# Attention block on one core: the odd head's queries and keys in six pairs formed from seven block products instead of eight

## The chip, the core and the metric

The kernel runs on one core of a Trainium2 chip. The metric is the device time of that core in microseconds (us). Three runs of the kernel before took 1060.37, 1062.02 and 1061.95 us, median 1061.95. Engines: PE multiplies matrices, DVE (VectorE), ACT (ScalarE) and POOL (GpSimd) work on elements, SP only issues transfers. Each engine executes its own instructions strictly in order and waits on semaphores.

## The reference, cut to what matters

```python
x = hidden_states                       # 2 x 512 tokens, 512 features, float32
n = layernorm(x)
q = rms_norm(n @ Wq + bq, gq)           # 32 heads of 128; the norm is over all 4096 columns
k = rms_norm(n @ Wk + bk, gk)
v = n @ Wv + bv
out = softmax(q k^T / sqrt(128)) v      # by head and batch
x = x + layernorm(out @ Wo + bo)
x = x + layernorm(gated_low_rank_ffn(layernorm(x)))
```

The change touches only `n @ Wq + bq` and `n @ Wk + bk` of some heads, and where sums of n are made.

## The kernel before, in words

Every product is made from float16 halves: a = a_hi + a_lo, and a product is hi x hi + hi x lo + lo x hi, so three matmuls for each 128-row chunk of the features. `xh` and `xl` hold the two halves of the normalised x, features on partitions, 4 chunks x 1024 tokens. Weights of a head (`wa_stage`, 4 slots, query and key) are scaled and split into `wa_hi` (ACT, L1119) and `wa_lo` (DVE, L2222).

The program has two phases. Phase A makes queries and keys of all 32 heads, in 16 pairs of an even and an odd head, and stores them in DRAM with the sums of their squares (`acc`). Phase B does the attention by pair. The norm needs the sums over all heads, so phase B can't begin before phase A is over. In the profile phase A ends near 345 us.

Phase A by head, on each engine (functions `phase_a`):
- PE: four items (`q_or_k`): query and key of batch 0, then of batch 1. An item is 4 chunks x 3 matmuls = 12 matmuls of 128x512 into one PSUM bank; even heads use banks 0 to 3, odd heads 4 to 7. PE waits for the weights (`wa_lo_ready`) and for the bank to be read (`k_out_ready`).
- ACT: for each item the squares; for query items also the scaled query in float32 (`q_s`) and its high half (`qk_out`); before the head, the high halves of the weights two heads on.
- DVE: the scale factors for two heads on (`next_factors`, nine small operations in a chain), the largest weight four heads on (`largest_qk`), the low halves of the weights (`low_wa`), the key of each batch (`store_k`), and the largest of one block of Wv or Wo (`largest_of_unit`).
- POOL: low half of the query (`low_q`) and two additions into `acc` for each batch.
- SP: loads of weights, stores of queries and keys.

Beside this POOL makes, two or four operations to a pair, four sums of blocks of x for phase B (`xs`, kinds XA, XE, XD, XG, each with a high and a low half). Phase B already makes most values from seven block products with them. They are made by pair 13 (36 operations, counted by `x_formed`) and first read in pair 2 of phase B. Nothing in phase A reads them.

Buffers set how far an engine may lag: one `squares` buffer and one `qk_out` buffer for the even head and one for the odd, four weight slots, one PSUM bank to an item.

## Time and profile before

| | |
|---|---|
| median of three runs | 1061.95 us |
| profiled execution | 1060.19 us |
| its span on the core | 1058.4 us |
| PE busy | 1039.7 us, 98% of the span |
| DVE, ACT, POOL busy | 828.2, 764.0, 763.4 us |
| PE idle from 0 to 420 us, longest waits | 1.8, 1.8 and 1.4 us, all in the first 15 us |

The span is the time from the first to the last recorded instruction. A matmul's recorded length (0.38 us) is longer than the distance between two starts, since matmuls overlap; how fast PE works is read from the starts. The same holds on the other engines to a smaller degree: the next start comes about 0.1 us before the recorded end.

### The profile page before, as it was taken

Reading aid. Unit: us, or ns where it says so; the run is one execution under the profiler, and the core shown is the slowest. Engines: PE = TensorE matmul, PEld = TensorE weight load, DVE = VectorE, ACT = ScalarE, POOL = GpSimd, SP = SyncE. Lnnn points to the kernel's source line nnn. Section 1 sums busy time; section 2 is a strip of 40 time slices with the busy share of each in tenths; the row PEclk is TensorE's granted clock in tenths of the full one; section 3 lists DMA queues with packets and bytes.
Section 4 is the critical chain, followed back from the end, with each engine's and each line's share of the span. In section 5 each row is a group of like instructions: output and inputs, shape, how many; then the busy total and the mean of one; then the engine's idle time right before and its main releaser. Section 6 shows DMA issues by size and latency. Waiting matters only on the chain.

```text
span 1058.4 us, 19677 instructions
## 1 busy us (share of the span) xinstructions
PE 1039.7 (98%) x5649; PEld 549.8 (52%) x5649; DVE 828.2 (78%) x1824; ACT 764.0 (72%) x1582; POOL 763.4 (72%) x717
## 2 busy tenths in 40 slices
PE   7999999999999999999999999999999999999997
PEld 4444444444444655556555555555555555555454
DVE  7777876667646778777887987888888888878887
ACT  4666766666647777776788787778787878877756
POOL 2687988788958577765777777778778778767313
PEclk9999999999999999999999999999999999999999
DMA  6678865656574569967667867876877987896702
GB/s 242 176 235 269 254 231 210 227 195 233 201 139 164 178 175 262 250 160 197 149 170 185 195 166 172 200 187 157 203 197 143 216 203 161 224 198 141 177 34 81
DMA packets 312761, 199.91 MB, mean 189 GB/s; under 512 B 275552, under 2 KB 279520, under 8 KB 312672
## 3 DMA queue, kind: packets, MB, share of 16 engines
q1 hardware_dynamic: 304752, 194.24, 68.1%
q10 hardware_dynamic: 7920, 4.62, 1.7%
q8 instruction: 39, 0.64, 0.2%
q14 instruction: 50, 0.41, 0.1%
HBM read 96.03 MB, written 35.68 MB: 124 GB/s over the span
## 4 chain that ended last, share of the span: by engine, by line
PE 87%; DVE 6%; ACT 3%; issue 1%; DMA 1%; POOL 1%; SPq 0%; DVEq 0%; ACTq 0%; POOLq 0%
PE ps L1621 26%; PE ps L1623 25%; PE ps L1622 25%; PE ps L1813 3%; PE ps L1814 3%; PE ps L1815 3%; ACT ps L1301 2%; DVE pair_q L2542 1%; ACT pair_q L1310 1%; DVE y L2555 1%; DMA pair_k<-pair_q 1%; DMA wa_stage<-w_qk 1%; DVE ps L2528 1%; DVE stats L2117 0%; PE ps L1733 0%
## 5 line engine op out<-in xcount | busy, mean ns | idle before, releaser
L1301 ACT ACTIVATE ps<-ps,neg_max 128x512 f32<-128x512 f32 x256 | 168.2, 657 | 57.7 <-DVE ps L2528 57.7
L2542 DVE SCALAR_TENSOR_TENSOR pair_q<-ps,row_inv,pair_q 128x512 f16<-128x512 f32 x256 | 174.2, 742 | 43.8 <-ACT pair_q L1310 40.4
L1621 PE MATMUL ps<-xh,wa_hi 128*128 128x512 f16 x512 | 194.1, 379 | 1.8 <-DVE wa_lo L2222 1.8
L1622 PE MATMUL ps<-xl,wa_hi 128*128 128x512 f16 x512 | 194.1, 379 | 0.0
L1623 PE MATMUL ps<-xh,wa_lo 128*128 128x512 f16 x512 | 194.1, 379 | 0.0
L2528 DVE TENSOR_SCALAR_CACHE_REDUCE ps<-ps,score_down 128x512 f32<-128x512 f32 x256 | 177.1, 753 | 15.2 <-PE ps L1623 14.5
L1310 ACT ACTIVATE pair_q<-ps,row_inv 128x512 f16<-128x512 f32 x256 | 154.5, 689 | 9.0 <-DVE row_inv L2535 8.8
L759 POOL TENSOR_TENSOR acc<-acc,squares 128x512 f32<-128x512 f32 x120 | 151.5, 1284 | 1.6 <-ACT squares L1152 1.6
L1152 ACT ACTIVATE squares<-ps,q_k_bias,qk_down 128x512 f32<-128x512 f32 x128 | 99.1, 785 | 42.9 <-PE ps L1623 28.6
L750 POOL TENSOR_TENSOR qk_out<-q_s,qk_out 128x512 f16<-128x512 f32 x64 | 75.5, 1181 | 52.4 <-ACT qk_out L1161 52.4
L2327 DVE TENSOR_SCALAR qk_out<-ps,k_b,k_g 128x512 f32<-128x512 f32 x64 | 51.8, 809 | 73.9 <-ACT squares L1152 73.8
L905 POOL TENSOR_TENSOR k_lo<-qk_in,k_hi 128x512 f16<-128x512 f32 x62 | 71.7, 1157 | 38.2 <-ACT k_hi L1258 38.1
L1621 PE MATMUL ps<-wo_hi,oth 128*128 128x512 f16 x256 | 97.1, 379 | 1.9 <-issue 0.9
L1621 PE MATMUL ps<-k_hi,qk_in 128*128 128x512 f16 x256 | 97.1, 379 | 1.2 <-issue 0.9
L1623 PE MATMUL ps<-wo_hi,otl 128*128 128x512 f16 x256 | 97.1, 379 | 0.0
L1622 PE MATMUL ps<-wo_lo,oth 128*128 128x512 f16 x256 | 97.1, 379 | 0.0
L1623 PE MATMUL ps<-k_hi,qk_in 128*128 128x512 f16 x256 | 97.1, 379 | 0.0
L1622 PE MATMUL ps<-k_lo,qk_in 128*128 128x512 f16 x256 | 97.0, 379 | 0.0
L1119 ACT ACTIVATE wa_hi<-wa_stage,qk_up 128x512 f16<-128x512 f32 x64 | 42.8, 718 | 75.0 <-DVE qk_up L2174 75.0
L936 POOL CAST oth<-o_t 128x512 f16<-128x512 f32 x62 | 38.3, 618 | 74.0 <-ACT o_t L1275 73.9
L1275 ACT ACTIVATE o_t<-ps,tab 128x512 f32<-128x512 f32 x62 | 42.7, 689 | 58.8 <-PE ps L1623 58.7
L1621 PEld LDWEIGHTS ps<-xh,wa_hi 128*128 128x128 f16 x512 | 50.3, 98 | 61.9 <-issue 2.1
(310 smaller groups left out, 2578.3 us busy)
## 6 DMA issues: line engine op xcount, KB each, us to landing
q_k_scratch<-qk_out SPq DMA_DIRECT2D x64, 512.0 KB, 4.0
qk_in<-q_k_scratch SPq DMA_DIRECT2D x64, 512.0 KB, 3.7
wa_stage<-w_qk SPq DMA_DIRECT2D x32, 512.0 KB, 4.2
u_stage<-w_vo SPq DMA_DIRECT2D x32, 512.0 KB, 5.3
wo_stage<-w_vo SPq DMA_DIRECT2D x16, 512.0 KB, 6.3
x_first<-w_vo SPq DMA_DIRECT2D x12, 512.0 KB, 4.4
qk_tops<-qk_top_scratch ACTq DMA_DIRECT2D x27, 128.0 KB, 3.5
pair_k<-pair_q SPq DMA_TRANSPOSE x130, 4.0
```

The source lines that it names most:

```text
L750: pool.tensor_tensor(pair(qk_out[:, par, b, 1, :])[:, 1, :], q_s[:, par, b * S:(b + 1) * S], pair(qk_out[:, par, b, 1, :])[:, 0, :], ALU.s ...
L759: pool.tensor_tensor(acc[:, w, cols], acc[:, w, cols], squares[:, par, w, cols], ALU.add).then_inc(acc_ready, 1)
L905: pool.tensor_tensor(k_lo[:, s % 2, :], qk_in[:, s, 0, :], k_hi[:, s % 2, :], ALU.subtract).then_inc(qk_lo_ready, 1)
L1152: act.activation(squares[:, par, w, b * S:(b + 1) * S], ps[:, 4 * par + g, :], ACT.Square, bias=q_k_bias[:, par, w:w + 1], scale=qk_down[: ...
L1301: act.activation(ps[:, SCORE + i, :], ps[:, SCORE + i, :], ACT.Exp, bias=neg_max[:, sl, i:i + 1], scale=-1.0, accum_out=row_sum[:, sl, i:i ...
L1310: act.activation(pair_q[:, 0, i, :], ps[:, SCORE + i, :], ACT.Identity, scale=row_inv[:, sl, i:i + 1]).then_inc(high_ready, 1)
L1621: pe.matmul(outp, lhs[0], rhs[0], start=first, stop=False)
L1622: pe.matmul(outp, lhs[0], rhs[1], start=False, stop=False)
L1623: return pe.matmul(outp, lhs[1], rhs[0], start=False, stop=last)
L2327: dve.tensor_scalar(qk_out[:, par, b, 0, :], ps[:, 4 * par + 2 * b + 1, :], k_b[:, slot:slot + 1], k_g[:, slot:slot + 1], ALU.add, ALU.mul ...
L2528: dve.tensor_scalar(ps[:, SCORE + i, :], ps[:, SCORE + i, :], score_down[:, sl, i:i + 1], None, ALU.mult, ALU.min, accum_out=neg_max[:, sl ...
L2542: dve.scalar_tensor_tensor(out=pair_q[:, 1, i, :], in0=ps[:, SCORE + i, :], scalar=row_inv[:, sl, i:i + 1], in1=pair_q[:, 0, i, :], op0=AL ...
```

## The change

**The products.** For the odd head of pairs 9 to 14, [Wk | Wq] is taken as a 2 x 2 block matrix (features 0 to 255 and 256 to 511; the query or the key) and x as 2 x 2 blocks too (features; tokens 0 to 255 or 256 to 511 of each batch). The four output blocks (query and key, first and second half of the tokens) come from seven products of sums of blocks rather than from eight products. A product is 2 chunks x 3 matmuls = 6 matmuls of 128x512. The seven are named C, A, E, B, D, G, F. They accumulate in PSUM banks 4 to 7, and partial results are copied from bank to bank by ACT and added by DVE. Both sums of weights of a formed head use one scale, so its factors are worked out by two dependent operations more.

**The order.** In these pairs the items of the even head lie between the products of the odd one: item, C, A, item, E, B, item, D, G, item, F. All other engines have a new written order for these pairs (`formed_pair`), in which the work of both heads is mixed.

**What each engine does in such a pair that it didn't do before.** POOL: four sums of weights (`formed_sums`, 512, 256, 256 and 256 elements). ACT: a scaled copy of product C to SBUF (`c_q`) and three copies of a bank to a bank, and for the weights one operation of 512 and one of 1280 elements in place of two of 512; two of `q_s` are gone. DVE: two operations that add `c_q` to the query's sums and write `q_s`, and for the weights one of 512 and one of 1280 in place of two of 512.

**The sums of x.** They are now read in pair 9 of phase A, so POOL makes them in pairs 1 to 8, four operations to a pair (30 instead of 36), and DVE makes the first steps of XG beside heads 7 to 11 (four differences of 512 elements and two additions of 512).

```diff
+        FIRST, LAST_PAIR = PAIRS // 2 + 1, PAIRS - 2
+        FORMED_A = LAST_PAIR - FIRST + 1
+        W_SUMS, COPIES, Q_SUMS, EXTRA = 4 * FORMED_A, 4 * FORMED_A, 2 * FORMED_A, 3 * FORMED_A
+        X_FORMS = 30
+        C_BANK, Q_LAST, Q_FIRST, K_BANK = 4, 5, 6, 7
+        f_sum = w_sum[:, :, :].rearrange("p a n -> p (a n)")[:, 0:10 * P]
+        f_parts = (w_form_a[:, :, :, :, :].rearrange("p a b c n -> p (a b c n)"),
+                   rms_row[:, :, :].rearrange("p a n -> p (a n)").bitcast(F16))
+        f_high = [part[:, 0:10 * P] for part in f_parts]
+        f_low = [part[:, 10 * P:20 * P] for part in f_parts]
+        c_q = k_lo[:, :, :].rearrange("p a n -> p (a n)").bitcast(F32)
...
+            def half(split, kind):
+                return lambda c: split(kind, of_first(c), c)
+            def high_half_g(c):
+                pool.wait_ge(x_by_dve, 6)
+                high_half(XG, two(qk_in[:, 2, c, :]), c)
+            def low_half_g(c):
+                low_half(XG, two(qk_in[:, 2, c, :]), c)
+            def formed_sums(h):
+                slot, f = h % 4, h // 2 - FIRST
+                pool.wait_ge(wa_loaded[slot], 16 * (h // 4 + 1))
+                if f > 0:
+                    pool.wait_ge(wa_lo_ready, 2 * h - 2)
+                w = wa_stage[:, slot]
+                pool.tensor_tensor(f_sum[:, 0:4 * P].rearrange("p (w c n) -> p w c n", w=2, c=2), w[:, :, 0:2, :],
+                                   w[:, :, 2:4, :], ALU.add).then_inc(w_formed, 1)
+                for k, one, other, op in ((F_E, w[:, 0, 0:2, :], w[:, 1, 2:4, :], ALU.add),
+                                          (F_F, w[:, 1, 0:2, :], w[:, 0, 0:2, :], ALU.subtract),
+                                          (F_C, w[:, 0, 2:4, :], w[:, 1, 2:4, :], ALU.subtract)):
+                    pool.tensor_tensor(f_block(f_sum, k).rearrange("p (c n) -> p c n", c=2), one, other,
+                                       op).then_inc(w_formed, 1)
...
+                if p < LAST_PAIR:
+                    formed_sums(h + 3)
+                low_q(0, 0, 2 * h + 1)
+                add_one(1, -1, 0, 0, batch(0))
+                add_one(2, 0, 0, 1, batch(0))
+                add_one(3, 2, 1, 1, tokens(0))
+                low_q(0, 1, 2 * h + 2)
+                add_one(4, 1, 0, 0, batch(1))
+                low_formed(0)
+                add_one(5, 4, 1, 0, tokens(0))
+                add_one(6, 3, 0, 1, batch(1))
+                low_formed(1)
+                add_one(7, 4, 1, 0, tokens(1))
+                add_one(8, 6, 1, 1, tokens(1))
...
-            phase_a(1, high_a)
-            phase_a(2, low_a)
-            phase_a(3, both_halves)
-            phase_a(4, split_a)
-            phase_a(5, high_e)
-            phase_a(6, low_e)
-            phase_a(7, split_e)
-            phase_a(8, high_d)
-            phase_a(9, low_d)
-            phase_a(10, split_d)
-            phase_a(11, high_and_low_g)
-            phase_a(12, both_halves)
-            phase_a(13, split_g)
-            phase_a(14)
+            phase_a(1, high_a, low_a)
+            phase_a(2, both_halves, half(high_half, XA))
+            phase_a(3, half(low_half, XA), high_e)
+            phase_a(4, low_e, half(high_half, XE))
+            phase_a(5, half(low_half, XE), high_d)
+            phase_a(6, low_d, half(high_half, XD))
+            phase_a(7, half(low_half, XD), high_half_g)
+            formed_sums(2 * FIRST + 1)
+            phase_a(8, low_half_g)
+            for p in range(FIRST, LAST_PAIR + 1):
+                formed_pair(p)
...
+            def high_formed(h):
+                slot, f = h % 4, h // 2 - FIRST
+                act.wait_ge(qk_up_ready, h + 1)
+                act.activation(corners(wa_hi[:, slot]), corners(wa_stage[:, slot]), ACT.Copy,
+                               scale=qk_up[:, slot, 0:1]).then_inc(wa_hi_ready, 1)
+                act.wait_ge(w_formed, 4 * f + 4)
+                act.activation(f_high[f % 2], f_sum, ACT.Copy,
+                               scale=qk_up[:, slot, 0:1]).then_inc(wa_hi_ready, 1)
...
+                act.wait_ge(q_sum_ready, 2 * f)
+                act.wait_ge(qk_product, products + 2)
+                act.activation(c_q, ps[:, C_BANK, :], ACT.Identity, bias=q_b[:, slots[1]:slots[1] + 1],
+                               scale=Q_DOWN).then_inc(v_copied, 1)
+                act.wait_ge(k_out_ready, 2 * h)
+                copy(K_BANK, 3)
+                high_wa(h + 2, (h + 2) % 4)
+                if p < LAST_PAIR:
+                    store_tops(h + 4, 0)
+                item(0, 1, slots[0], products + 4)
+                copy(Q_FIRST, 5)
+                act.wait_ge(bias_ready, h + 2)
+                squared(3)
+                square_key(0, 6)
+                if p < LAST_PAIR:
+                    load_tops(h + 4, 0)
+                    high_formed(h + 3)
+                else:
+                    high_wa(h + 3, (h + 3) % 4)
+                act.wait_ge(acc_ready, 4 * h + 4)
+                act.wait_ge(stored[0][1], 16 * p)
+                item(0, 2, slots[0], products + 7)
+                act.wait_ge(k_out_ready, 2 * h + 2)
+                copy(K_BANK, 8)
+                for b in range(2):
+                    act.wait_ge(stored[1][b], 16 * p)
+                squared(5)
+                formed_query(0)
+                if p < LAST_PAIR:
+                    store_tops(h + 5, 1)
+                act.wait_ge(acc_ready, 4 * h + (6 if f else 4))
+                item(0, 3, slots[0], products + 10)
+                squared(7)
+                formed_query(1)
+                squared(8)
+                square_key(1, 11)
...
+                pe.wait_ge(wa_lo_ready, 2 * h + 1)
+                pe.wait_ge(k_out_ready, 2 * h - 3)
+                q_or_k(0, 0, slots[0])
+                pe.wait_ge(wa_lo_ready, 2 * h + 4)
+                pe.wait_ge(k_out_ready, 2 * h - 1)
+                product(W_C, C_BANK, True)
+                if f:
+                    pe.wait_ge(q_sum_ready, 2 * f)
+                else:
+                    pe.wait_ge(x_formed, X_FORMS)
+                product(W_A, Q_LAST, True)
+                q_or_k(0, 1, slots[0])
+                pe.wait_ge(v_copied, 4 * f + 2)
+                product(W_E, Q_LAST, False)
+                product(W_B, K_BANK, False)
+                q_or_k(0, 2, slots[0])
+                pe.wait_ge(v_copied, 4 * f + 3)
+                product(W_D, Q_LAST, False)
+                product(W_G, Q_FIRST, False)
+                q_or_k(0, 3, slots[0])
+                pe.wait_ge(v_copied, 4 * f + 4)
+                product(W_F, K_BANK, False)
...
+                if formed:
+                    dve.tensor_scalar(qk_most[:, slot, 0:1], qk_most[:, slot, 0:1], qk_most[:, slot, 1:2],
+                                      least_q[:, h:h + 1], ALU.max, ALU.max).then_inc(qk_down_ready, 1)
+                    dve.wait_ge(qk_down_ready, 2 * h + 1)
+                    dve.tensor_scalar(qk_down[:, slot, :], qk_most[:, slot, 0:1].broadcast_to([P, 2]), 1.0 / W_UP,
+                                      None, ALU.mult).then_inc(qk_down_ready, 1)
...
+            def half_g(half, c, to):
+                dve.tensor_tensor(by_half(qk_in[:, to, c, :]), over_tokens(half[:, 2 + c, :], 0),
+                                  over_tokens(half[:, 2 + c, :], 1), ALU.subtract).then_inc(x_by_dve, 1)
...
+                next_factors(h + 2, 0, (h + 2) % 4)
+                top(h)
+                low_wa(h + 2, (h + 2) % 4)
+                unit(h + 2)
+                dve.wait_ge(k_cols_ready, 3 * h + 3)
+                dve.wait_ge(stored[0][0], 16 * p)
+                store_k(0, 0, slots[0], 8 * p + 2)
+                next_factors(h + 3, 1, (h + 3) % 4, p < LAST_PAIR)
+                dve.wait_ge(k_cols_ready, 3 * h + 6)
+                for b in range(2):
+                    dve.wait_ge(stored[1][b], 16 * p)
+                formed_key(0, 8 * p + 3)
+                top(h + 1)
+                unit(h + 3)
+                if p < LAST_PAIR:
+                    low_formed(h + 3)
+                else:
+                    low_wa(h + 3, (h + 3) % 4)
+                if more:
+                    more()
+                dve.wait_ge(qk_product, products + 9)
+                for second, bank in enumerate((Q_FIRST, Q_LAST)):
+                    dve.wait_ge(v_copied, 4 * f + 3 + second)
+                    dve.scalar_tensor_tensor(out=over_tokens(q_s[:, 1, :], second), in0=by_half(ps[:, bank, :]),
+                                             scalar=Q_DOWN, in1=by_half(c_q), op0=ALU.mult,
+                                             op1=ALU.add).then_inc(q_sum_ready, 1)
+                dve.wait_ge(stored[0][1], 16 * p)
+                store_k(0, 1, slots[0], 8 * p + 6)
+                formed_key(1, 8 * p + 8)
```

In pairs 1 to 14 before, PE has 12 matmuls after 12 matmuls, and waits only at an item's start. The last item of one trip of the loop and the start of the next:

```order
L1621 MATMUL ps<-xh,wa_hi 128x512
L1622 MATMUL ps<-xl,wa_hi 128x512
L1623 MATMUL ps<-xh,wa_lo 128x512
L1714 UNCONDITIONAL_BRANCH [waits qk_down_ready]
L1714 ISA
L1704 REGISTER_ALU [waits wa_lo_ready]
L1621 MATMUL ps<-xh,wa_hi 128x512 [waits k_out_ready]
L1622 MATMUL ps<-xl,wa_hi 128x512
L1623 MATMUL ps<-xh,wa_lo 128x512
```

Now, in pair 9, the end of the first item, product C (its weights are called `w_form_a`) and the start of product A (`xs` are the sums of x, `wa_hi` and `wa_lo` the weights' own blocks):

```order
L1817 MATMUL ps<-xh,wa_hi 128x512
L1818 MATMUL ps<-xl,wa_hi 128x512
L1819 MATMUL ps<-xh,wa_lo 128x512
L1938 MATMUL ps<-xh,w_form_a 128x512 [waits k_out_ready,wa_lo_ready]
L1939 MATMUL ps<-xl,w_form_a 128x512
L1940 MATMUL ps<-xh,w_form_a 128x512
L1938 MATMUL ps<-xh,w_form_a 128x512
L1939 MATMUL ps<-xl,w_form_a 128x512
L1940 MATMUL ps<-xh,w_form_a 128x512
L1938 MATMUL ps<-xs,wa_hi 128x512 [waits x_formed]
L1939 MATMUL ps<-xs,wa_hi 128x512
L1940 MATMUL ps<-xs,wa_lo 128x512
```

What moved: after each item come one or two products of six matmuls, and three new waits stand in PE's row: C waits for the formed weights of this head and for a key of the pair before, A for the sums of x in pair 9 (later for the query sums of the pair before), E, D and F for ACT's copies.

DVE in the loop before, from the split of weights to the next head's factors:

```order
L2222 SCALAR_TENSOR_TENSOR wa_lo<-wa_stage,qk_up,wa_hi 128x512 [waits wa_hi_ready] x2
L2327 TENSOR_SCALAR qk_out<-ps,k_b,k_g 128x512 [waits k_cols_ready,stored1_0,sq_ready]
L2335 TENSOR_REDUCE vo_top<-u_stage 128x1 [waits u_loaded1]
L2327 TENSOR_SCALAR qk_out<-ps,k_b,k_g 128x512 [waits stored1_1,sq_ready]
L2207 TENSOR_REDUCE qk_most<-qk_tops 128x2 [waits qk_tops_loaded]
```

DVE now, in pair 9, from the odd head's first key (L2724) on; L2494 and L2498 split the weights of head 21 (`rms_row` is where the low halves lie every other pair), L2751 makes the query sums (`k_lo` holds `c_q`):

```order
L2724 TENSOR_SCALAR qk_out<-ps,k_b,k_g 128x2x256 [waits stored1_1,sq_ready,stored1_0,k_cols_ready]
L2411 TENSOR_REDUCE qk_top<-wa_stage 128x2 [waits wa_loaded3]
L2610 TENSOR_REDUCE vo_top<-u_stage 128x1 [waits u_loaded1]
L2494 SCALAR_TENSOR_TENSOR wa_lo<-wa_stage,qk_up,wa_hi 128x2x256 [waits wa_hi_ready]
L2498 SCALAR_TENSOR_TENSOR rms_row<-w_sum,qk_up,rms_row 128x1280 [waits wa_hi_ready]
L2751 SCALAR_TENSOR_TENSOR q_s<-ps,k_lo 128x2x256 [waits v_copied,qk_product]
L2751 SCALAR_TENSOR_TENSOR q_s<-ps,k_lo 128x2x256 [waits v_copied]
L2602 TENSOR_SCALAR qk_out<-ps,k_b,k_g 128x512 [waits sq_ready,stored0_1]
L2724 TENSOR_SCALAR qk_out<-ps,k_b,k_g 128x2x256 [waits sq_ready]
```

What moved: the two L2751, which wait for product G and ACT's copy, stand behind the split of 512 and 1280 elements, and ahead of the even head's second key (L2602) and the odd head's second (L2724), on which PE waits at the start of the next pair.

ACT now, in pair 9, from the split of the formed sums (L1310) to the pair's end; L1350 is the copy of bank to bank, L1361 and L1363 square and round the query sums (`step_to` holds their scale), L1354 squares the odd head's key:

```order
L1310 ACTIVATE rms_row<-w_sum,qk_up 128x1280 [waits w_formed]
L1257 ACTIVATE squares<-ps,q_k_bias,qk_down 128x512 [waits qk_product,stored0_1,acc_ready]
L1264 ACTIVATE q_s<-ps,q_b 128x512
L1266 ACTIVATE qk_out<-ps,q_b 128x512
L1350 ACTIVATE ps<-ps 128x512 [waits qk_product,k_out_ready]
L1361 ACTIVATE squares<-q_s,step_to 128x2x256 [waits acc_ready,q_sum_ready,stored1_1,stored1_0]
L1363 ACTIVATE qk_out<-q_s 128x2x256
L1291 DMA qk_top_scratch<-qk_top 128x2 [waits qk_top_ready]
L1257 ACTIVATE squares<-ps,q_k_bias,qk_down 128x512 [waits qk_product,acc_ready]
L1361 ACTIVATE squares<-q_s,step_to 128x2x256 [waits q_sum_ready,acc_ready]
L1363 ACTIVATE qk_out<-q_s 128x2x256
L1354 ACTIVATE squares<-ps,q_k_bias,qk_down 128x2x256 [waits qk_product,acc_ready]
```

What moved: two squares and two high halves of the odd head wait for DVE (`q_sum_ready`), and the even head's last key item stands between them.

## Rows read from the trace of the kernel before

**Rows 1.** The page's busy times by engine.

```profile
PE 1039.7 (98%) x5649; PEld 549.8 (52%) x5649; DVE 828.2 (78%) x1824; ACT 764.0 (72%) x1582; POOL 763.4 (72%) x717
```

**Rows 2.** Stretches: PE, PEld, DVE, ACT, POOL busy us, clock, DMA share, GB/s.

```profile
50.00:150.00 100.00, 100.00 (x465) 45.33 (x464) 74.87 (x143) 66.66 (x111) 87.93 (x72) 1.00 0.77 248
200.00:320.00 120.00, 120.00 (x557) 54.24 (x556) 75.49 (x155) 74.30 (x123) 96.31 (x82) 1.00 0.62 196
```

**Rows 3.** Timeline of PE in head 18: start us, us; 50 matmuls lie between.

```profile
205.57 0.38 PE L1623 MATMUL ps<-xh,wa_lo 128*128 128x512 f16 x1
...
216.58 0.38 PE L1623 MATMUL ps<-xh,wa_lo 128*128 128x512 f16 x1
```

**Rows 4.** Timeline of ACT in head 18; in brackets the idle time before.

```profile
207.39 1.34 ACT L1119 ACTIVATE wa_hi<-wa_stage,qk_up 128x512 f16<-128x512 f32 x2 [1.91 <-DVE qk_up L2174]
...
209.39 0.78 ACT L1152 ACTIVATE squares<-ps,q_k_bias,qk_down 128x512 f32<-128x512 f32 x1 [0.57 <-ACT q_k_bias L1146]
210.07 0.68 ACT L1159 ACTIVATE q_s<-ps,q_b 128x512 f32<-128x512 f32 x1
...
211.20 0.79 ACT L1152 ACTIVATE squares<-ps,q_k_bias,qk_down 128x512 f32<-128x512 f32 x1
...
215.06 0.78 ACT L1152 ACTIVATE squares<-ps,q_k_bias,qk_down 128x512 f32<-128x512 f32 x1 [0.66 <-PE ps L1623]
```

**Rows 5.** Timeline of ACT in pair 15, where no loop register is read.

```profile
334.29 0.24 ACT L1146 ACTIVATE q_k_bias<-tab 128x2 f32<-128x2 f32 x1
334.56 0.78 ACT L1152 ACTIVATE squares<-ps,q_k_bias,qk_down 128x512 f32<-128x512 f32 x1
```

**Rows 6.** Timeline of DVE in head 18.

```profile
206.24 0.41 DVE L2207 TENSOR_REDUCE qk_most<-qk_tops 128x2 f32<-128x256 f32 x1
...
209.22 1.41 DVE L2222 SCALAR_TENSOR_TENSOR wa_lo<-wa_stage,qk_up,wa_hi 128x512 f16<-128x512 f32 x2
212.02 0.81 DVE L2327 TENSOR_SCALAR qk_out<-ps,k_b,k_g 128x512 f32<-128x512 f32 x1 [1.39 <-ACT squares L1152]
212.75 1.21 DVE L2335 TENSOR_REDUCE vo_top<-u_stage 128x1024 f32 x1
```

**Rows 7.** Timeline of POOL in head 18.

```profile
214.97 1.15 POOL L750 TENSOR_TENSOR qk_out<-q_s,qk_out 128x512 f16<-128x512 f32 x1
216.09 2.48 POOL L759 TENSOR_TENSOR acc<-acc,squares 128x512 f32<-128x512 f32 x2
218.54 1.15 POOL L776 TENSOR_TENSOR qk_in<-qk_in,xl 128x512 f32<-128x512 f32 x1
```

**Rows 8.** Durations by line, ns min/median/max: how they grow with the elements.

```profile
L2486 DVE SCALAR_TENSOR_TENSOR y<-ps,y_down,y x10: 735/741/748, 392.0 to 1004.0; 128x512 f32<-128x512 f32 x10
L2555 DVE SCALAR_TENSOR_TENSOR y<-ps,y_down,y x55: 1265/1272/1277, 430.5 to 982.8; 128x1024 f32<-128x1024 f32 x55
L1324 ACT ACTIVATE ps<-ps x66: 365/376/385, 468.3 to 913.3; 128x256 f32<-128x256 f32 x66
```

**Rows 9.** Timeline of DVE, the split for head 9.

```profile
108.06 2.76 DVE L2222 SCALAR_TENSOR_TENSOR wa_lo<-wa_stage,qk_up,wa_hi 128x512 f16<-128x512 f32 x2
```

**Rows 10.** Timeline of POOL, heads 7 to 10.

```profile
108.55 1.72 POOL L776 TENSOR_TENSOR qk_in<-qk_in 128x512 f32<-128x512 f32 x1
110.32 1.51 POOL L750 TENSOR_TENSOR qk_out<-q_s,qk_out 128x512 f16<-128x512 f32 x1
...
130.16 1.16 POOL L750 TENSOR_TENSOR qk_out<-q_s,qk_out 128x512 f16<-128x512 f32 x1
```

**Rows 11.** Groups by line: the DVE split at 50 to 150, then 200 to 320.

```profile
L2222 DVE SCALAR_TENSOR_TENSOR wa_lo<-wa_stage,qk_up,wa_hi 128x512 f16<-128x512 f32 x20 | 20.9, 1084 | 0.0
L2222 DVE SCALAR_TENSOR_TENSOR wa_lo<-wa_stage,qk_up,wa_hi 128x512 f16<-128x512 f32 x23 | 20.2, 916 | 0.1
```

**Rows 12.** Durations by line on DVE, ns min/median/max.

```profile
L2542 DVE SCALAR_TENSOR_TENSOR pair_q<-ps,row_inv,pair_q x256: 732/741/752, 355.9 to 998.6; 128x512 f16<-128x512 f32 x128
L2428 DVE TENSOR_SCALAR score_down<-rms,exp_scale x64: 215/230/1226, 345.7 to 987.9; 128x5 f32<-128x5 f32 x64
```

294 lines of the change are left out of this document (219 added, 75 removed).

## The prediction

> **What bounds the kernel now.** First the page's busy line: PE works 98% of the span, the others 72 to 78% [rows 1]. Then the stretches, since a share over the whole span hides phases: in the two stretches of phase A that end before pair 15, PE is busy all of the time at a granted clock of 1.00, its 2.4 GHz level [rows 2]. Then PE's own row: from 205.57 to 216.58 lie 51 starts, 0.216 us each [rows 3]. So phase A is a queue of matmuls with no gap, an item of 12 takes 2.59 us, a head 10.35, a pair 20.7. Last, the slack of the others in a head. I read what an operation occupies as the distance to the next start. ACT: square 0.68, a scaled copy 0.57 (two in 1.13), a split of weights 0.62 [rows 4]. DVE: factors and largest weight together 2.98, of which the reduction is 1.12 like the one of 1.21 us recorded, so 1.86 for the factors; split 0.70 each, key 0.73 [rows 6]. POOL: low half 1.12, addition 1.23 each, a sum of x 1.15 [rows 7]. POOL is the fullest: 87.9 of 100 us [rows 2].
>
> **What it removes.** A formed head has 7 x 6 = 42 matmuls for 48. Six pairs: 36 x 0.216 = 7.8 us off PE, if PE stays without a gap. That is the whole possible gain. A formed pair would take 90 x 0.216 = 19.4 us. No transfer is added.
>
> **What it adds, off PE.** Per formed pair:
> - POOL: 8 additions 9.8, 4 low halves 4.5, the sums of weights. No row has a POOL sum of 256 elements; between half of 1.23 and all of it the four cost 3.1 to 4.9. I take 3.1, in proportion to the elements. Sum 17.4 of 19.4.
> - ACT: 8 squares 5.4, four even and two odd query copies 3.4, `c_q` and three bank copies 2.3, the even head's weights 1.2, the formed ones. Two bracketing rows of one operation on DVE, 741 ns for 512 and 1272 for 1024 elements, give 1.04 ns an element [rows 8]; ACT's bank copy of 256 takes 376 ns beside 680 for 512 [rows 4, 8], 1.2 ns an element at most, so 1280 elements take 1.4 to 1.6. Sum near 14.7.
> - DVE: factors 1.7 (unrolled) and 1.9, two largest weights 2.2, even split 1.4, two units 2.2, four keys 2.9, formed split 0.70 + 1.5, query sums 1.4. Sum 16.0.
>
> Each fits in 19.4. But the order ties them together, so the question is a loop, not a sum.
>
> **The loop.** Let T be when ACT ends a pair's last square (odd key, after product F), counted from PE's start of the next pair. From T on: the next pair's first square starts 0.16 later (bias to square is 0.27 without loop registers [rows 5]); square and two copies 1.8, bias 0.2, `c_q` 0.57, copy to the key's bank 0.57 ends at T+3.4; the even weights' high half is there at T+4.1. DVE then: split 1.4, unit 1.12, even key 0.73, formed factors 1.9, odd key 0.73, largest 1.12, unit 1.12, formed split 0.70 + 1.5, first query sum 0.74: T+15.2. Back to ACT: square and copy 1.24, even key's square 0.68, square and copy 1.24, last square 0.8: T+19.2. The loop is 19.2 us, just under PE's 19.4. It has no room for anything else.
>
> PE is held when T is over 3.6: product C waits for the even head's second key, which DVE ends at T-1.1, and C stands 2.59 into the pair; product E waits for T+3.4 and stands at 7.8, so T may be 4.3 there. The first of these is what ends last. When PE isn't held, T is at least 1.9: the even key's square can't end before 8.8, and from there the same chain runs 12.5 to the end.
>
> **What doesn't fit: two engines that stop each other.** The DVE split of 2 x 512 takes 1.41 us when POOL has little to do [rows 6], but 2.76 at 108.06 [rows 9], while POOL's next two operations took 1.72 and 1.51 [rows 10] rather than about 1.25 and 1.15. Its mean is 1084 ns at a POOL share of 0.88, and 916 at 0.80 [rows 2, 11], against 741 for the same kind on PSUM data, whose spread is 732 to 752 over 256 of them [rows 12]. So it is operations with two SBUF inputs that pay, 0.35 to 0.7 us for two of them on average, 1.35 at most. In a formed pair there are four such (two splits of two), and POOL's share is 17.4/19.4 = 0.90. I take the row nearest to that share, 0.7 for two: c = 1.4 in a pair. Bounds: 0, and 2.7. The query sums have a PSUM input and pay nothing. The scale of 128x2 elements, new, may pay as `score_down` of 128x5 does (215 to 1226 ns [rows 12]); I take nothing and keep it for the range.
>
> The Trainium skill, page "SBUF — State Buffer", section "SBUF: two separate sides", says that DVE with two SBUF inputs and a reading GpSimd operation take one port pair as an exclusive lock for the whole instruction, and the later one fully blocks. By that rule the trace agrees: the rows show whole waits, not a common slowing. It speaks against this change, which loads both engines at once; what it would make of the time is the second rival.
>
> **The sum.** Loop with c: 19.2 + 1.4 = 20.6, so T grows by 1.2 a pair until PE is held. Pair 9 starts near T = 1.0. There another wait comes first: product A needs the last sum of x. In head 18 POOL's last sum ended at 219.69 [rows 7], and the last square, which waited for PE, began at 215.06 [rows 4], so PE was done about 214.8: 4.9 behind PE. In head 17 now ACT and DVE are 1.0 later for the formed split, and POOL, which made 3.1 us of sums of weights at the start of pair 8 with 2.0 spare, some 0.7 late more. 6.6 against 3.9, where A stands: 2.7 us of a hole, once. Then T is 1.9 + 0.7 = 2.6 at pair 10, 3.8 at 11 (held 0.2), 4.8 at 12, 13 and 14 (held 1.2 each). Holes: 2.7 + 0.2 + 3.6 = 6.5. Behind pair 14, which has no formed split and no largest weights to find, T is back under 3 and pair 15 starts as before. Removed 7.8, given back 6.5: 1.3 us gained. 1060.19 becomes 1058.9; the median of the runs is 1.76 above the profiled one, so 1060.7.
>
> **Pairs 1 to 8** cost nothing, if POOL keeps up: with two operations to a head, from 110.32 to 130.16 it did two heads in 19.84, 9.9 a head [rows 10], of 10.35. One of those two was a cast, about half an addition; heads with two real sums need some 0.5 more, just PE's pace, in pairs 1, 3 and 5 only. The `squares` buffers let POOL lag by most of a head. DVE's extra six operations there (0.7 to 1.4 each) lie in 25% idle time [rows 2]. If that cover is gone, POOL's lag goes into the hole of pair 9.
>
> **Rivals.**
> 1. The locks cost half (0.35 for two, as at the share 0.80 [rows 11]) because POOL stands idle, waiting for ACT's query halves, just when DVE splits. For: in the written order POOL's low half waits behind the query sums, and the formed split lies ahead of these. Against: POOL's additions of the pair before run to T+4.5 and the sums of weights from there, right over the even split at T+4.1. Then c = 0.7, T: 2.3, 2.8, 3.3, 3.8, 4.1; held 0.2 + 0.5, the hole 2.0 for a POOL on time. 7.8 - 2.7 = 5.1 gained: 1056.9.
> 2. Slower: DVE behind POOL, at `low_wa` and `low_formed`, once per operation. With POOL never idle each waits half of an addition to a whole one, 0.6: c = 2.4. T: 3.1, 5.3, then 5.8: held 1.7 + 3 x 2.2, and 2.7: 11.0 - 7.8 = 3.2 lost, 1065.2. With the maximum 2.7 and 0.4 for the scale, 6 lost. It decides from c = 1.8 on, where the six pairs take as long as before. For: rows 9 are of such a moment. Against: in most heads less was paid. This is the case that the skill's lock rule gives when taken strictly.
> 3. POOL falls behind in pairs 1 to 8 (two sums a head, all contended at 1.7, 10.5 a head), comes 3 us later to its last sum, and the hole of pair 9 is 5.5: 9.3 - 7.8 = 1.5 lost, 1063.5.
>
> **Chances.** Forecast 0.36, rival 1 0.31, rival 2 0.25, rival 3 0.08. What a measurement here can tell from no change is 0.2%, 2.1 us. Faster by more: 0.09 of the forecast's and 0.30 of rival 1: 0.39. Slower: 0.21 of rival 2, 0.03 of rival 3, 0.02 of the forecast: 0.26. Within: 0.35. The range for 8 in 10 leaves out a gain of over 5.5 and a loss of over 5: 1056.4 to 1067.0. The likeliest case alone: 1058.7 to 1063.
>
> **What would show it.** Holes on PE in front of product C of pairs 11 to 14, released by DVE's key, 0.2 then about 1.2 us; none in front of D and F. One hole before A in pair 9, released by POOL, 2 to 3.5 us. Split operations on DVE near 1.1 us (the 512) and 2.0 (the 1280). A pair period near 20.6 in pairs 11 to 13. If PE runs without a gap from pair 10 on, the loop was priced too long (rival 1); if periods pass 21.2, too short (rival 2). Holes before pair 9 would be rival 3. The prediction fails outright if phase B changes by more than 1 us, or if PE's start distance in the products isn't 0.216.

## The result, and the profile after

The changed kernel takes 1080.3 us (median of four runs, 1078.73 to 1080.88) beside 1061.99 for the one before: ratio 1.0170, interval 1.0151 to 1.0189. The forecast was 1060.7, its range ended at 1067.0. The profiled execution took 1078.73, its span is 1076.9, 18.5 more than before.

The page's busy line, in answer to [rows 1]:

```profile
PE 1040.6 (97%) x5613; PEld 548.5 (51%) x5613; DVE 864.6 (80%) x1848; ACT 770.4 (72%) x1594; POOL 796.8 (74%) x735
```

PE has 36 matmuls less and 0.9 us more of busy time: that is work at a lower clock. The stretches show where, in answer to [rows 2] (window, its length, then PE, PEld, DVE, ACT, POOL busy, clock, DMA share, GB/s):

```profile
100.00:150.00 50.00, 50.00 (x233) 22.69 (x232) 45.41 (x77) 32.96 (x56) 49.64 (x38) 1.00 0.70 237
200.00:225.00 25.00, 16.99 (x68) 7.03 (x67) 12.15 (x18) 10.80 (x21) 22.94 (x20) 0.80 0.53 179
225.00:250.00 25.00, 25.00 (x118) 11.33 (x117) 21.29 (x43) 16.86 (x28) 20.27 (x17) 1.00 0.64 198
275.00:300.00 25.00, 22.86 (x99) 9.78 (x97) 19.56 (x34) 16.05 (x27) 21.77 (x17) 0.93 0.70 182
300.00:325.00 25.00, 20.76 (x89) 8.72 (x88) 18.25 (x31) 13.12 (x22) 19.09 (x17) 0.93 0.70 157
```

From 100 to 200 us PE has no gap, but POOL has hardly one either (99.2 of 100 us busy). What PE waited for until 420 us (in total, times, longest):

```profile
PE ps L1938 <- POOL xs L841: 8.0, 1, 8.0
PE ps L1938 <- DVE qk_out L2602: 4.5, 4, 2.1
PE ps L1938 <- ACT ps L1350: 4.0, 2, 3.8
```

All are in front of products of formed heads. The first, in pair 9 before product A, and what follows it (start, recorded length), in answer to [rows 3]:

```profile
208.56 0.38 PE L1940 MATMUL ps<-xh,w_form_a 128*128 128x512 f16 x1
216.95 0.61 PE L1938 MATMUL ps<-xs,wa_hi 128*128 128x512 f16 x1 [8.01 <-POOL xs L841]
217.35 0.63 PE L1939 MATMUL ps<-xs,wa_hi 128*128 128x512 f16 x1
...
221.62 0.63 PE L1819 MATMUL ps<-xh,wa_lo 128*128 128x512 f16 x1
222.04 0.46 PE L1817 MATMUL ps<-xh,wa_hi 128*128 128x512 f16 x1
222.34 0.38 PE L1818 MATMUL ps<-xl,wa_hi 128*128 128x512 f16 x1
```

Twelve matmuls start 0.43 apart, at the 1.2 GHz level, and only then 0.216 again: 2.5 us on top of the hole. The same stands behind two of the holes of pairs 12 and 13. Measured from start to start, which gives some more than the waits listed above, the holes in pairs 9 to 14 sum to 17.9 us, and the slow matmuls to about 6.1. Less the 7.8 removed that is 16.2. The first sum of columns, the end of phase A, starts at 358.3, before at 341.8, 0.4 of which was lost in the first 15 us. From the last sum of columns (381.1, before 364.7) to the end it is 695.8 us, before 693.7: 2.1 are lost in phase B, whose work is unchanged.

POOL at that hole, in answer to [rows 7], the last sum of x (L841) behind the additions (L824) of pair 8's last squares:

```profile
208.64 1.15 POOL L815 TENSOR_TENSOR qk_out<-q_s,qk_out 128x512 f16<-128x512 f32 x1
209.75 2.48 POOL L824 TENSOR_TENSOR acc<-acc,squares 128x512 f32<-128x512 f32 x2
212.19 1.15 POOL L815 TENSOR_TENSOR qk_out<-q_s,qk_out 128x512 f16<-128x512 f32 x1
213.30 2.48 POOL L824 TENSOR_TENSOR acc<-acc,squares 128x512 f32<-128x512 f32 x2
215.74 1.15 POOL L841 TENSOR_TENSOR xs<-qk_in,xs 128x512 f16<-128x512 f32 x1
```

The longest stall of the loop is in pair 13, and PE's hole there, 3.8 us in front of product B, waits for ACT's copy of a bank (L1350). DVE and ACT in that pair, in answer to [rows 6, 4]; each wait in brackets stands before the operation:

```profile
306.17 3.32 DVE L2486 SCALAR_TENSOR_TENSOR wa_lo<-wa_stage,qk_up,wa_hi 128x512 f16<-128x512 f32 x2
...
316.31 0.81 DVE L2724 TENSOR_SCALAR qk_out<-ps,k_b,k_g 128x512 f32<-128x512 f32 x1 [2.79 <-DMA q_k_scratch<-qk_out]
...
319.92 1.22 DVE L2610 TENSOR_REDUCE vo_top<-u_stage 128x1 f32<-128x1024 f32 x1 [1.63 <-DMA u_stage<-w_vo]
```

```profile
306.06 0.34 ACTq L1291 DMA_DIRECT2D qk_top_scratch<-qk_top  x1
...
316.76 0.72 ACT L1307 ACTIVATE wa_hi<-wa_stage,qk_up 128x512 f16<-128x512 f32 x1 [6.38 <-DMA qk_top_scratch<-qk_top]
...
325.52 0.72 ACT L1361 ACTIVATE squares<-q_s,step_to 128x512 f32<-128x512 f32 x1 [4.48 <-DVE q_s L2751]
```

A store of 1 KB, issued at 306.06, landed only after 10.2 us. From 310 us on the transfer engines were busy and moved little (the last two figures are their share and GB/s):

```profile
310.00:312.00 2.00, 2.00 (x11) 0.93 (x10) 1.84 (x4) 0.38 (x1) 2.00 (x4) 1.00 1.07 104
312.00:314.00 2.00, 2.00 (x11) 0.88 (x10) 1.34 (x8) 0.00 (x0) 2.00 (x3) 1.00 1.12 78
```

### The profile page after: what moved, and what is told of

It reads as the page before. It is cut to its first block, busy times and chain, and to the rows that moved or that the text cites. A ratio compares the mean times of both kernels' runs of the same rounds, so it can differ in the third digit from the quotient of the medians.

```text
span 1076.9 us, 19041 instructions
## 1 busy us (share of the span) xinstructions
PE 1040.6 (97%) x5613; PEld 548.5 (51%) x5613; DVE 864.6 (80%) x1848; ACT 770.4 (72%) x1594; POOL 796.8 (74%) x735
## 4 chain that ended last, share of the span: by engine, by line
PE 62%; POOL 14%; DVE 10%; ACT 6%; issue 5%; DMA 2%; ACTq 0%; SPq 0%; DVEq 0%; POOLq 0%
PE ps L1817 17%; PE ps L1819 17%; PE ps L1818 17%; POOL acc L824 7%; POOL qk_out L815 3%; PE ps L2066 3%; PE ps L2068 3%; PE ps L2067 3%; ACT ps L1497 2%; POOL qk_in L841 2%; DVE pair_q L2890 2%; DMA qk_top_scratch<-qk_top 1%; POOL xs L841 1%; PE ps L1938 1%; ACT pair_q L1506 1%
## 5 line engine op out<-in xcount | busy, mean ns | idle before, releaser
L1817 PE MATMUL ps<-xh,wa_hi 128*128 128x512 f16 x416 | 158.5, 381 | 0.2 <-DVE wa_lo L2486 0.2
L1818 PE MATMUL ps<-xl,wa_hi 128*128 128x512 f16 x416 | 158.4, 381 | 0.0
L1819 PE MATMUL ps<-xh,wa_lo 128*128 128x512 f16 x416 | 158.3, 380 | 0.0
L1257 ACT ACTIVATE squares<-ps,q_k_bias,qk_down 128x512 f32<-128x512 f32 x104 | 79.9, 784 | 29.5 <-PE ps L1819 19.0
L824 POOL TENSOR_TENSOR acc<-acc,squares 128x512 f32<-128x512 f32 x72 | 99.8, 1407 | 1.6 <-ACT squares L1257 1.6
L815 POOL TENSOR_TENSOR qk_out<-q_s,qk_out 128x512 f16<-128x512 f32 x52 | 66.0, 1271 | 24.2 <-ACT qk_out L1266 24.0
L1004 POOL TENSOR_TENSOR qk_in<-qk_in,rms_row 128x512 f32<-128x512 f32 x62 | 78.9, 1272 | 0.6 <-ACT rms_row L1459 0.6
L2486 DVE SCALAR_TENSOR_TENSOR wa_lo<-wa_stage,qk_up,wa_hi 128x512 f16<-128x512 f32 x52 | 67.8, 1342 | 12.3 <-ACT wa_hi L1224 12.1
L1043 POOL TENSOR_TENSOR otl<-o_t,oth 128x512 f16<-128x512 f32 x62 | 71.6, 1155 | 5.0
```

The lines of the kernel that those rows point to most:

```text
L815: pool.tensor_tensor(pair(qk_out[:, par, b, 1, :])[:, 1, :], q_s[:, par, b * S:(b + 1) * S], pair(qk_out[:, par, b, 1, :])[:, 0, :], ALU.s ...
L824: pool.tensor_tensor(acc[:, w, cols], acc[:, w, cols], squares[:, par, w, cols], ALU.add).then_inc(acc_ready, 1)
L1004: pool.tensor_tensor(qk_in[:, s, 0, :], qk_in[:, s, 0, :], factors(b), ALU.mult).then_inc(qk_scaled, 1)
L1257: act.activation(squares[:, par, w, b * S:(b + 1) * S], ps[:, 4 * par + g, :], ACT.Square, bias=q_k_bias[:, par, w:w + 1], scale=qk_down[: ...
L1817: pe.matmul(outp, lhs[0], rhs[0], start=first, stop=False)
L1818: pe.matmul(outp, lhs[0], rhs[1], start=False, stop=False)
```

## The experiments

Ratios are to the kernel before, run on the same chip. Where two versions are compared, two ratios are subtracted, each known to about 0.2% (2 us). So a gain of 4 us stands only just clear of the noise, and one of 5 or 6 us does more safely. A profile shows one run, which can lie some us from the median. "A to D" is the time from the first matmul of product A in pair 9 to the last product D of pair 14: 122.6 us in the changed kernel (216.9 to 339.5). Line numbers shift a little from kernel to kernel.

**The load of POOL** (a1, a5). In a1:

```diff
+            pool.memset(xs[:, :, :, :, :], 0.37).then_inc(x_formed, 1)
...
-                pool.tensor_tensor(dst, src, other, op).then_inc(x_formed, 1)
+                pool.tensor_tensor(dst[:, :, 0:8], src[:, :, 0:8], other[:, :, 0:8], op).then_inc(x_formed, 1)
```

> The 30 sums and splits of x on POOL in pairs 1 to 8 are cut to 16 of their 512 elements (xs is filled with a constant instead, so the products of the odd heads of pairs 9 to 14 and of the values are of other numbers). Theory 1 (POOL fell behind by these 30 instructions, and that made the hole of 8.0 us before product A in pair 9 and the 12 matmuls at half clock behind it, 2.5 us): the hole is under 1 us, about 10.5 us go, 1080.3 to about 1070. Rival (the loop of ACT and DVE in the formed pairs is the bound, and what the hole no longer takes is taken by pairs 9 to 14): the hole goes, but the time falls by less than 4 us, to 1076 or more.

Ratio 1.0156. The hole was 1.3, but the fill stood ahead of the first roots on POOL and shifted the start by some 5 us, so the total says little, and the short hole as little: product A started at 215.76, only 1.2 us sooner than in the changed kernel. A to D fell to 119.0. a5 has no fill at the start. Its sums are as small, and the halves are constants:

```diff
-                pool.tensor_copy(two(xs[:, 0, kind, c, :]), src).then_inc(x_formed, 1)
+                pool.memset(xs[:, 0, kind, c, :], 0.37).then_inc(x_formed, 1)
...
-                form_x(two(xs[:, 1, kind, c, :]), src, two(xs[:, 0, kind, c, :]), ALU.subtract)
...
+                pool.memset(xs[:, 1, kind, c, :], 0.0001).then_inc(x_formed, 1)
```

> As in the first run of this kind the sums of x on POOL are made small (the sums 16 elements wide, the halves constants of full width), but nothing is added at the start, where that run's fill of xs held POOL and cost PE 3.8 us. Theory 1 (POOL behind by the sums of x): the hole before product A is under 1 us, and product A of pair 9 starts 7 to 8 us sooner, at about 209; against the changed kernel 9 to 11 us go, a ratio to the kernel before of 1.007. Rival (the loop in the formed pairs takes it back): product A starts sooner, but the last product of xs in pair 14 comes less than 4 us sooner, ratio over 1.013.

Ratio 1.0198, interval 1.0175 to 1.0222: no gain, so the theory that POOL's load alone makes the loss fell. POOL (wait in brackets) shows why:

```profile
207.47 1.85 POOL L815 TENSOR_TENSOR qk_out<-q_s,qk_out 128x512 f16<-128x512 f32 x1 [0.71 <-ACT qk_out L1268]
...
212.85 2.48 POOL L824 TENSOR_TENSOR acc<-acc,squares 128x512 f32<-128x512 f32 x2
215.27 0.52 POOL L863 MEMSET xs<- 128x512 f16 x1
```

POOL isn't late here, it waits for ACT; still the last operation on xs comes at 215.27, since it stands behind the additions, and PE waits 5.2 us. Product A started at 215.85, 1.1 us sooner; A to D was 123.1, 0.5 longer.

**The place of the last sum** (a6): in pair 8 ahead of the head's work.

```diff
+                    for one in ahead:
+                        one(par)
                     for b in range(2):
...
-            phase_a(8, low_half_g)
+            phase_a(8, ahead=(low_half_g,))
```

> In pair 8 POOL makes the head's low half of x ahead of its query halves and additions, not behind them; nothing is left out. Theory 1b (with the sums cut small the hole before product A was still 5.2 us, since the last sum stood behind the additions of pair 8's last squares, which ACT delivers only after PE is done with the pair: it is the place that makes the hole, at least as much as the load): the last sum ends at about 209.8 instead of 216.9, the hole is under 1.5 us, no slow matmuls behind it, product A at about 210.5. Whether that stays: if the loop of the formed pairs is the bound, it gives back more than half, and the ratio is 1.012 to 1.015; if not, 1.008. Rival (POOL's load alone): the hole stays over 5 us, since everything is only in another order.

Ratio 1.0132, interval 1.0113 to 1.0151, 4 us less. The hole is 2.4 instead of 8.0 and product A starts 5.5 us sooner, so the place of the last sum made most of that hole. A to D was 126.3, 3.7 longer: over half given back, as expected of a loop that binds. How much exactly stays open, because this profile took 1079.43, 3.4 above the median of its runs.

**The locks** (b4): the sums of weights are made in full only for the first formed head; for the others they are cut to 16 columns of each block.

```diff
+                n = 2 * P if f == 0 else 8
...
-                                   w[:, :, 2:4, :], ALU.add).then_inc(w_formed, 1)
...
+                                   w[:, :, 0:2, 0:n // 2], w[:, :, 2:4, 0:n // 2], ALU.add).then_inc(w_formed, 1)
...
```

> POOL's sums of the weights are full only for the first formed head (for the other five they are 16 columns of each block wide, so that head 19's sums stand in for them). Theory 2 with the lock (DVE's splits of 743 ns take 1344 to 1650 in formed pairs since POOL's sums of two operands run beside them): DVE's low halves of the formed pairs fall back to near 743 and 1850 ns, the loop gets 1 to 2 us shorter in each of five pairs, 5 us of the holes and slow matmuls of pairs 10 to 14 go, ratio 1.012. Rival (POOL's other work beside the splits keeps them as long, or the loop is bound by ACT's waits): the splits stay over 1200 ns, under 1.5 us go, ratio 1.0155 or more. The hole of pair 9 stays.

Ratio 1.0202, no gain. Splits in pairs 9 to 14, changed kernel, then b4 (count, busy, mean ns):

```profile
L2486 DVE SCALAR_TENSOR_TENSOR wa_lo<-wa_stage,qk_up,wa_hi 128x512 f16<-128x512 f32 x12 | 18.1, 1544 | 12.1 <-ACT wa_hi L1224 11.9
```

```profile
L2487 DVE SCALAR_TENSOR_TENSOR wa_lo<-wa_stage,qk_up,wa_hi 128x512 f16<-128x512 f32 x12 | 12.6, 1087 | 11.5 <-ACT wa_hi L1225 11.4
```

The sums of weights do lengthen these splits, by 457 ns each, 5.5 us in all. A to D fell by only 1.6, while the wait for a transfer in pair 13 happened to be longer (ACT 8.0 instead of 6.4) and the hole before A too (9.4). So the locks cost something in the loop, but they aren't the main cause. Their exact price isn't shown.

**DVE's order** (a2): the two query sums stand ahead of the formed split (the moved block is cut here):

```diff
+                dve.wait_ge(qk_product, products + 9)
+                for second, bank in enumerate((Q_FIRST, Q_LAST)):
...
                 if p < LAST_PAIR:
                     low_formed(h + 3)
...
-                dve.wait_ge(qk_product, products + 9)
-                for second, bank in enumerate((Q_FIRST, Q_LAST)):
...
                 dve.wait_ge(stored[0][1], 16 * p)
                 store_k(0, 1, slots[0], 8 * p + 6)
```

> In each pair from 9 to 14 DVE makes the odd head's two query sums before its low halves of the formed weights, not behind them. Theory 2 (DVE's row is full from the even head's split to the query sums, 241.8 to 255.2 in pair 10, and ACT's last square waits for it): the pair's end comes 1.5 us sooner each time, of the 9.3 us of holes in pairs 10 to 14 and the 3.6 us of slow matmuls behind them about half goes: 1074. Rival (ACT's wait for the transfers of the tops sets the pair's end): ACT still stands 2.5 and 6.4 us before its high halves, less than 2 us go: 1078.5 or more. Neither touches the hole of 8.0 us in pair 9.

Ratio 1.0119, interval 1.0102 to 1.0136: 5.4 us less, A to D 116.5. DVE's row in pair 10, the changed kernel and then a2:

```profile
252.46 1.55 DVE L2498 SCALAR_TENSOR_TENSOR w_form_a<-w_sum,qk_up,w_form_a 128x1280 f16<-128x1280 f32 x1
253.92 1.28 DVE L2751 SCALAR_TENSOR_TENSOR q_s<-ps,k_lo 128x512 f32<-128x512 f32 x2
256.73 0.81 DVE L2602 TENSOR_SCALAR qk_out<-ps,k_b,k_g 128x512 f32<-128x512 f32 x1 [1.53 <-ACT squares L1257]
```

```profile
251.38 0.68 DVE L2745 SCALAR_TENSOR_TENSOR q_s<-ps,k_lo 128x512 f32<-128x512 f32 x1
252.84 0.69 DVE L2745 SCALAR_TENSOR_TENSOR q_s<-ps,k_lo 128x512 f32<-128x512 f32 x1 [0.78 <-ACT ps L1350]
...
256.59 0.80 DVE L2602 TENSOR_SCALAR qk_out<-ps,k_b,k_g 128x512 f32<-128x512 f32 x1
```

The first sum comes 2.5 us sooner, and ACT's squares of the query sums, which had waited 1.5 us for DVE, don't wait.

**Transfers.** a3, on ACT:

```diff
                 if p < LAST_PAIR:
-                    load_tops(h + 4, 0)
                     high_formed(h + 3)
...
                 item(0, 2, slots[0], products + 7)
+                if p < LAST_PAIR:
+                    load_tops(h + 4, 0)
```

> In pairs 9 to 13 ACT's load of the even head's tops, which waits until their store has landed, stands behind the third group of the even head, not ahead of the odd head's high halves. Theory 3 (that wait, 6.4 us in pair 13 and 2.5 us in pairs 10 and 12, holds ACT's row and makes the hole of 4.0 us in pair 13 and its slow matmuls): 4 to 6 us go, 1075. Rival (DVE's full row is what is late, ACT's wait stands beside it): under 2 us, 1078.5 or more.

Ratio 1.0190, interval 1.0170 to 1.0209: nothing gained. The rival held: DVE waited for a store in the same pair (3.4 us), whatever ACT did. a7 moves SP's loads ahead of the stores:

```diff
-                weights(h)
-                load_unit(h + 3, 1, h + 3)
+                if p == FIRST:
+                    weights(h)
+                    load_unit(h + 3, 1, h + 3)
...
                 if p < LAST_PAIR:
                     load_unit(h + 4, 0, h + 4)
+                    weights(h + 2)
+                    load_unit(h + 5, 1, h + 5)
                 sp.wait_ge(k_out_ready, 2 * h + 3)
```

> In formed pairs SP issues the next pair's first loads of weights and of a value unit ahead of the stores of the pair's last three blocks, not behind them; nothing is left out. Theory 3b (the two stores of the odd head and two loads, 512 KB each, are issued within 3 us at the pair's end; the store of 304.88 lands after 11.4 us at 316.31 and holds DVE, the tops' store of 306.06 lands at 316.37 and holds ACT): DVE's wait for the store in pair 13 (2.8 us), for u_stage (1.6 us) and ACT's for the tops (6.4 us) go or halve, the hole of 4.0 us before product B of pair 13 is under 1.5 us: 4 to 6 us less, ratio 1.012. Rival (DVE's row is full, transfers only fill its gaps): the waits go and the pair's period stays over 21 us, less than 2 us gained, 1.0155 or more.

Ratio 1.0216, interval 1.0192 to 1.0241: slower. The rival's bound holds, but not its reason: the waits didn't go, and ACT's for the tops in pair 13 was 7.8. That loads ahead of the stores make the stores late is my reading of it. This order didn't cure the bunching. But one thing was the same in every run up to here: from pair 10 on, the longest wait for a transfer, 3.4 to 8.0 us, stood in the pair behind the store of the values' tops (`vo_top_scratch<-top_v`, 128 x 4 bytes). a8 moves this store to pair 7, with the reduction on DVE that makes its values:

```diff
+                if i == 4:
+                    sp.wait_ge(v_top_ready, 1)
+                    sp.dma_start(vo_top_scratch[0], top_v[:, :]).then_inc(v_top_stored, 16)
                 for o in range(-2, 2):
                     phase_a(i, o)
...
+            largest_value()
...
-            largest_value()
```

> The largest value weights (128 x 4 bytes, vo_top_scratch) are reduced, stored and read back in pairs 7 and 8, not in pairs 12 to 14; nothing is left out. Theory 5 (this store is what fills the transfer engines at under 110 GB/s from 310 to 316 us, so that the odd head's store and the tops' store behind it land after 10 to 11 us; the long stall of every version with formed pairs stands right behind it): DVE's and ACT's waits in pair 13 fall to 2.5 us or less, the hole of 4.0 us before product B of pair 13 and its slow matmuls go, 4 to 6 us less than the changed kernel, ratio 1.012. Rival (the two stores of the odd head and the two loads bunched at each pair's end do it, and pair 13 only has the bad luck to come last): the stall in pair 13 stays over 4 us, under 2 us gained, 1.0155 or more.

Ratio 1.0112, interval 1.0095 to 1.0128: 6.2 us less, A to D 116.2, and in pair 13 neither DVE nor ACT waits for a transfer. From 310 to 316 us the transfers moved 201 to 303 GB/s instead of 78 to 104. They crept at the store's new place instead: issued at 171.19, it was followed from 174 to 180 us by 37 to 45 GB/s, where PE waited for nothing. a9 makes the store once more, between pairs 10 and 11, and takes DVE's reduction there from its place ahead of pair 13:

```diff
+                if p == 11:
+                    sp.wait_ge(v_top_ready, 1)
+                    sp.dma_start(vo_top_scratch[1], top_v[:, :]).then_inc(v_top_stored, 16)
                 formed_pair(p)
...
+                if p == 11:
+                    largest_value()
                 formed_pair(p)
-            largest_value()
```

> The same store twice: once more, into the other row of the scratch, between pairs 10 and 11; nothing is left out. Theory 5: pair 11 gets the stall that pair 13 has (ACT's wait for the tops' store over 5 us, in place of none in pair 11), a hole before its product B of 2 to 4 us with slow matmuls, 3 to 6 us more, ratio 1.021. Rival (bunching alone): no change, 1.017.

Ratio 1.0215, interval 1.0193 to 1.0238: 4.8 us more, A to D 127.9. ACT in pairs 11 and 13:

```profile
275.88 0.72 ACT L1310 ACTIVATE wa_hi<-wa_stage,qk_up 128x512 f16<-128x512 f32 x1 [7.55 <-DMA qk_top_scratch<-qk_top]
...
323.14 0.72 ACT L1310 ACTIVATE wa_hi<-wa_stage,qk_up 128x512 f16<-128x512 f32 x1 [6.80 <-DMA qk_top_scratch<-qk_top]
```

Taken away the stall goes, doubled it comes twice, from 268 to 274 us at 39 to 76 GB/s. The stall of pair 13 stays though DVE's reduction no longer stands there, so it is the store and not the reduction. In the kernel before the same store was issued at 290.00, and the transfers crept just so, but PE waited for nothing:

```profile
294.00:296.00 2.00, 2.00 (x11) 0.88 (x9) 1.02 (x2) 1.60 (x3) 1.65 (x2) 1.00 0.57 23
296.00:298.00 2.00, 2.00 (x11) 0.93 (x10) 0.91 (x1) 1.34 (x4) 2.00 (x3) 1.00 1.08 39
```

**Together.** a267 is a2, a6 and a7; a268 is a2, a6 and a8.

> The last sum ahead, the loads ahead and the query sums ahead together, all six pairs formed, nothing left out. If the three causes (place of POOL's last sum, transfers bunched at a pair's end, DVE's order) make up the loss, holes in pairs 9 to 14 sum to under 5 us in place of 17.9 and slow matmuls to under 2 us: 14 to 18 us less than the changed kernel, ratio 1.000 to 1.004. If a fourth limit stands behind them (DVE's work of 18 us per formed pair with the locks, against PE's 19.4), the ratio stays over 1.007.

Ratio 1.0094, interval 1.0069 to 1.0120. It missed 1.004 and passed the mark of 1.007 set for a fourth limit. But a268, which has a8 where this has a7, is 8.4 us faster, so what stood behind was the transfers and not DVE's amount of work. a2 with a6 alone wasn't run.

> The query sums ahead, the last sum of x ahead, and the tops of the values early, six pairs formed, loads as in the changed kernel. If these are the three causes: no hole over 3 us in pairs 9 to 14, holes and slow matmuls together under 8 us of the changed kernel's 24, ratio 1.003. If bunched transfers alone hold the loop: 1.007 or more.

Ratio 1.0015, interval 1.0005 to 1.0025: 16.5 us less than the changed kernel; the three alone gave 5.4, 4.0 and 6.2, 15.6. No matmul at the slow level, A to D 113.5. Left until 420 us:

```profile
PE ps L1940 <- DVE qk_out L2604: 5.0, 5, 1.9
PE ps L1940 <- ACT ps L1352: 0.6, 1, 0.6
PE ps L1940 <- POOL xs L843: 0.4, 1, 0.4
```

a52 is a2 on a5.

> The small sums of x and the query sums ahead of the low halves together. If the two are independent, their gains add: 10 us and 5 us of the changed kernel's 18 go, ratio 1.003. If DVE, POOL and ACT slip into one another's row once PE comes sooner, the second gain is under 2 us: 1.007 or more.

Ratio 1.0131: 7.1 us less than a5 alone. The gain of a2 is there again, that of a5 is not: the result fits neither of the two numbers expected.

**Fewer formed pairs.** a4 forms pairs 11 to 14 and spreads the sums of x over ten pairs (two a head to pair 5, then one). a24 adds a2 to it, a2467 also a6 and a7, a2468 a6 and a8.

```diff
-        FIRST, LAST_PAIR = PAIRS // 2 + 1, PAIRS - 2
+        FIRST, LAST_PAIR = 11, PAIRS - 2
```

> Only pairs 11 to 14 are formed (24 matmuls fewer than before, not 36), and the 30 instructions on x are spread over pairs 1 to 10 (two per head up to pair 5, then one). Theory 1: POOL keeps up (9.9 to 10.9 us per head against PE's 10.4, and catches up in pairs 6 to 10), the hole of 8.0 us and its 2.5 us of slow matmuls go, 2.6 us of matmuls come back, two pairs of the loop fewer: about 1069. Rival (POOL can't recover, or the loop is what counts): a hole of more than 3 us before product A of pair 11, 1075 or more.

> Formed pairs 11 to 14 alone, with the query sums ahead of the low halves. Pairs from 11 have the hole of 2.3 us before product A and 7.8 us of holes in the loop with their slow matmuls; the loop's part halves, 4 to 5 us go against the run with pairs 11 to 14 alone: ratio 1.010. If what binds there is ACT's bank copy (2.4 us waited for), under 2 us go: 1.0135 or more.

> The same three edits with pairs 11 to 14 formed alone and the sums of x spread over pairs 1 to 10. Two formed pairs fewer cost 2.6 us of matmuls and save two rounds of the loop: if no limit is left it is 2 to 3 us behind the version with six pairs, ratio 1.000 to 1.005; if the loop of ACT and DVE still binds, it is the faster of the two.

> The same with pairs 11 to 14 alone formed and the sums of x over pairs 1 to 10. The version of this kind with the loads ahead had one hole of 4.6 us and one of 1.6 us with 11 slow matmuls, about 8.5 us in all; by theory 5 5 to 7 us of that go: ratio 0.999 to 1.002. By the rival it stays at 1.005.

Ratios 1.0152, 1.0131, 1.0059, 1.0010 (interval 0.9998 to 1.0023). a4 missed 1069 us: with the hole down to 2.3, 7.8 us of holes released by DVE's keys and ACT's bank copy remained. a24's interval (1.0089 to 1.0173) is too wide to tell. a2467 is 3.7 us faster than a267 with its six pairs, as expected if the loop still binds. In a2468 phase A ends at 338.7, 3.1 us sooner than before, and phase B gives 5.2 back.

**Phase B.** The five versions with formed pairs whose phase B I read (changed, a4, a8, a268, a2468) have this on DVE, here the changed kernel:

```profile
706.13 0.76 DVE L2876 TENSOR_SCALAR_CACHE_REDUCE ps<-ps,score_down 128x512 f32<-128x512 f32 x1
706.80 0.15 DVE L2876 DVE_READ_ACCUMULATOR ps<-ps,score_down 128x1 f32 x1
709.69 0.76 DVE L2876 TENSOR_SCALAR_CACHE_REDUCE ps<-ps,score_down 128x512 f32<-128x512 f32 x1 [2.75 <-issue]
```

It is the fourth of four equal operations at the head of the second round of phase B's loop, and nothing that the profile shows released it. Phase A's code on DVE is longer now (1010 instructions ahead of that loop, before 814).

```diff
+            for _ in range(30):
+                dve.sem_inc(begun, 1)
             store_k(0, 0, 2, 8 * PAIRS - 6)
...
+            for _ in range(31):
+                dve.sem_inc(begun, 1)
             low_wv(0, 0)
```

> The last version (pairs 11 to 14 formed, query sums, last sum and tops of the values moved) with 61 semaphore increments that nobody waits for in DVE's row where phase A ends, 30 and 31 of them ahead of the last two keys of the phase, where DVE waits 2.7 us for ACT each time; nothing is left out. Theory 6: every version with formed pairs has a wait of DVE of 2.2 to 2.8 us ('issue': nothing released it) among four equal score operations at the start of the second round of phase B's loop, which the kernel before hasn't, because the longer straight code of phase A has moved the loop to another place in DVE's program (a transfer of instructions is 0.64 MB / 39 = 16 KB in the profile); 61 instructions more put it where it stood, if such blocks hold 256 instructions. Then the wait goes, PE's waits behind it (2.7 us for ACT's copy and 0.5) too: 3 to 4 us less than without them, ratio 0.998. Rival (the wait is from phase B's own transfers, wherever the code stands): DVE's issue wait stays over 2 us, ratio 1.001 to 1.002.

> The kernel before, with 196 such increments in DVE's row of phase A, 16 or 20 behind each of twelve heads, and nothing else: its loop of phase B then stands in DVE's program where that of the changed kernel stands. Theory 6: DVE gets an issue wait of 2.2 to 2.8 us at the start of the loop's second round, about 330 to 350 us behind the first sum of columns, and PE some 2 us of waits behind it; phase A keeps its time: 2 to 3 us more than the kernel before, ratio 1.002 to 1.003. Rival: no such wait, ratio 0.999 to 1.001.

a2468_shift: ratio 0.9983, interval 0.9973 to 0.9993, twelve runs, the fastest of all, though a2468_shift's phase A ends 2.0 us later than a2468's. The issue wait is gone. c_before_shift: ratio 1.0040, interval 1.0026 to 1.0053, with an issue wait of 2.45 us at the same four operations. The stretch of 50 us that begins 300 us behind the last sum of columns: before, c_before_shift, a2468, a2468_shift (PE busy is the third figure, behind the window and its length):

```profile
664.70:714.70 50.00, 49.10 (x279) 27.01 (x277) 41.88 (x89) 37.64 (x88) 39.43 (x39) 1.00 0.79 180
```

```profile
669.80:719.80 50.00, 47.36 (x267) 25.63 (x265) 37.72 (x87) 36.30 (x85) 37.67 (x37) 1.00 0.85 189
```

```profile
661.50:711.50 50.00, 46.97 (x257) 25.30 (x256) 36.63 (x79) 34.74 (x79) 34.57 (x35) 0.97 0.82 184
```

```profile
663.60:713.60 50.00, 49.66 (x281) 27.25 (x280) 39.85 (x90) 38.21 (x89) 40.31 (x40) 1.00 0.80 178
```

The shift costs the kernel before 1.7 us there and gives a2468 2.7. The rest of c_before_shift's loss lies ahead of that loop: its sums of columns begin 1.7 us later and take 3.4 longer. I put this to the increments themselves, which isn't shown, and so its total can't be read as the price of the place. a2468 had another 2.1 us of PE waits earlier in phase B that a2468_shift lacks; whether they hang on the place too is open.

## Why the prediction was wrong

The forecast gave back 6.5 us of 7.8. The traces give:

| given back, us | forecast | measured |
|---|---|---|
| hole before A in pair 9 | 2.7 | 8.2 |
| holes in the later pairs | 3.8 | 9.7 |
| matmuls at the 1.2 GHz level | 0 | 6.1 |
| start of phase A, and phase B | 0 | 0.4 + 2.1 |

The first two measured figures are the 17.9 above, from start to start. The sum is 26.5; less 7.8 it is 18.7 beside the 18.5 of the two spans.

- **Removed: 7.8.** Right where PE runs at 0.216; the condition "without a gap" failed.
- **The hole of pair 9, 2.7.** Right place and releaser, wrong size: 8.0. The step took POOL to be 0.7 late from the sums of weights. It was late from pair 2 on and hardly ever idle (49.64 of 50), because "9.9 a head" came from a stretch with a cast; heads with two real sums took 10.6 to 11.2. Rival 3 had this and priced it at 5.5. And the load is only a part: a5 kept a hole of 5.2 with hardly any load, and a6 cut it to 2.4 by the place alone. The step had the releaser right and didn't ask what stood ahead of the last sum in POOL's row.
- **The loop, 19.2 + 1.4.** The measured periods (ACT's last squares: 258.43, 280.50, 302.28, 329.22) are 22.1, 21.8 and 26.9. This is the step that failed: the loop was summed from instructions alone. "No transfer is added" was true, but the waits for the transfers that were there had no term. In pair 13 the store of the values' tops cost 6.2 us by a8, and 4.8 once more by a9, and the hole that it made stood in front of B, where none was listed. The sum of 19.2 also left every other wait without room: DVE's order, which was in it as written, is worth 5.4 by a2.
- **The locks, c = 1.4.** Too small. Two splits took up to 3.3 against 1.41, more than the 2.76 of [rows 9] taken as the most. The even split took 1.6 more than two uncontended ones (743 ns each, as most splits of 512 in L2494 took), and the split of 1280 took either 1.55 or some 2.5, so c was about 2.3 in a pair, near rival 2's 2.4. The Trainium skill, page "SBUF — State Buffer", section "SBUF: two separate sides", says that one of the two engines blocks the other for a whole instruction. The trace agrees in kind (1544 against 1087 ns when POOL's sums are small), but b4, which took 0.9 of this c from a pair's even split, got 1.6 us in all for it. So rival 2 had the size of c nearly right, and c didn't set the time.
- **No price for the clock.** After holes of 8.0, 2.1 and 3.8 us PE ran some 12, 8 and 9 matmuls at 0.43: 6.1 us, a quarter of the 24 lost in these pairs (the gains of a2, a6 and a8 contain their shares of it). In a268, with holes up to 1.9 us, no matmul was slow. The length of the hole doesn't settle it alone: in a6 slow matmuls followed a hole of 2.4 us at 211.49, and none one of 3.3 us at 326.82.
- **Phase B unchanged.** A change of over 1 us was named as what would make the prediction fail outright, and it changed by 2.1. The code's length had no term.
- **The range.** The range ended 6.3 us above the forecast, since its width was made from the locks and POOL's lag alone. Each row of the table missed by less than that, and all of them together by 20.0.

## What to carry to other kernels

A chain of engines that closes just under the period of the engine that bounds the kernel (19.2 of 19.4) has no room, and a wait that hid in slack before becomes time. Price its transfers and small stores, not only its instructions. A hole costs more than its length where the clock falls behind it. When the first use of a value is near, look first at where its last producer stands in that engine's row, and only then at the engine's load.

## What the runs showed of the hardware

- Four us after a store of 128 x 4 bytes to one row of DRAM was issued among the usual 512 KB transfers, these crept for about 6 us: 23 to 39 GB/s in the kernel before (294 to 300 us), 78 to 104 in the changed one (310 to 316), 37 to 45 in a8, 39 to 76 in a9, at transfer engine shares of 0.4 to 1.4. A 1 KB store behind it landed after 10.2 us. Why so small a store does this is not shown.
- 196 semaphore increments in phase A gave the kernel before a wait of 2.45 us in phase B, and 61 took one of 2.6 us out of another. So the place of the loop in the engine's code matters for the start of its second round. I chose 61 because 196 + 61 = 257: if the code is fetched in blocks of 256 instructions, as the expectation assumed, 61 put the loop back to within one instruction of its old place in a block. The profile gives 0.64 MB / 39 = 16 KB for a transfer of instructions. Two kernels fit that; it is no proof of the number.
